# Attention's 32 bodies written as a hardware loop of seven passes and a tail of four

## The reference

```python
x = L0_attn_x                                  # (2, 2048, 256), float32
xn = _layernorm(x, axis=-1)
x = x + mamba(xn) + ffn(xn)
# inside ffn, with 16 heads of width 16:
scores = jnp.einsum('bhqd,bhkd->bhqk', q, k) / jnp.sqrt(jnp.float32(D))
attn = jax.nn.softmax(scores, axis=-1)
o = jnp.einsum('bhqk,bhkd->bhqd', attn, v)
x = x + (o @ wo + bo)
hn2 = _layernorm(x, ln2_g, ln2_b).reshape(-1, h)
idx = jnp.argmax(hn2 @ gate_w + gate_b, axis=-1)
moe = y[idx, jnp.arange(hn2.shape[0])]         # y: relu feed-forward of each of 8 experts
```

## Time and profile before

| | |
|---|---|
| median of 3 executions | 3217.68 us (3217.47 to 3218.07) |
| the profiled execution | 3217.68 us |
| its span, first to last instruction | 3215.9 us |
| instructions in it | 37482 |
| busy in attention, 1433.7 to 2637.7 us (1204.0 us) | PE 1188.9, DVE 1163.0, ACT 881.5, POOL 80.2 us |
| granted TensorE clock, mean | 0.943 |

### The profile page before, as it was taken

The page is one execution under the profiler, slowest core; times in us unless marked ns, Lnnn a source line. Parts: engine busy times, 40 slices in busy tenths (PEclk is TensorE's granted clock), DMA queues, the critical chain, the costliest instruction groups (busy, mean ns, idle before and its releaser), DMA issues. The chain is left out here.

```text
span 3215.9 us, 37482 instructions
## 1 busy us (share of the span) xinstructions
PE 2883.6 (90%) x13148; PEld 1472.8 (46%) x13148; DVE 2647.9 (82%) x4268; ACT 1706.1 (53%) x2088; POOL 981.1 (31%) x554
## 2 busy tenths in 40 slices
PE   5768899898898775899999999999999998859998
PEld 3423344343343332444444444444444442648887
DVE  8819999999999996799999999999999994642222
ACT  3435564565655632067777777777777777101111
POOL 3506565565565565101101101011010000344443
PEclk9889999999999987599999999999999999769999
DMA  7731121221221222835555545555554420655663
GB/s 202 182 104 60 63 83 72 80 84 60 74 89 68 73 72 30 109 46 74 84 71 78 77 62 75 67 82 84 71 77 63 63 31 29 96 137 193 202 210 107
DMA packets 206598, 288.18 MB, mean 90 GB/s; under 512 B 113437, under 2 KB 154038, under 8 KB 191948
## 3 DMA queue, kind: packets, MB, share of 16 engines
q1 hardware_dynamic: 195052, 260.22, 39.1%
q0 software_dynamic: 11360, 25.62, 2.7%
HBM read 237.34 MB, written 53.36 MB: 90 GB/s over the span
## 5 line engine op out<-in xcount | busy, mean ns | idle before, releaser
L782 DVE TENSOR_REDUCE attn_mx<-attn_pX 128x1 f32<-128x512 f32 (+1 forms) x2560 | 1305.0, 576 | 72.5 <-PE attn_pX L687 32.2
L758 ACT ACTIVATE attn_pr<-attn_pS 128x1024 f32<-128x1024 f32 x1024 | 991.6, 1021 | 447.1 <-PE attn_pS L699 447.0
L687 PE MATMUL attn_pX<-attn_ks,attn_qs 48*128 48x512 f32 (+1 forms) x2560 | 899.7, 439 | 46.2 <-DMA attn_vs<-v_d 25.0
L687 PEld LDWEIGHTS attn_pX<-attn_ks,attn_qs 48*128 48x128 f32 x2560 | 446.7, 189 | 667.6 <-DVE attn_mx L782 562.7
L1221 PE MATMUL mamba_pY<-mamba_g,mamba_ident 128*128 128x512 f32 x1024 | 520.1, 655 | 136.7 <-DVE mamba_g L1369 136.5
L699 PE MATMUL attn_pS<-attn_qs,attn_ks 50*128 50x512 f32 x2048 | 626.0, 437 | 3.6 <-ACT attn_pr L758 3.6
L1349 DVE TENSOR_TENSOR_SCAN mamba_h<-mamba_pA,mamba_hs,mamba_db 128x512 f32<-128x512 f32 x512 | 616.9, 1263 | 13.5 <-ACT mamba_pA L1071 13.2
L1007 POOL TENSOR_TENSOR mamba_db<-mamba_bq,mamba_u 128x2048 f32<-128x2048 f32 x128 | 580.2, 4533 | 63.2 <-DVE mamba_u L1310 63.2
L1071 ACT ACTIVATE mamba_pA<-mamba_dt,held_an 128x512 f32<-128x512 f32 x512 | 352.5, 691 | 389.6 <-DVE mamba_h L1349 389.1
L709 PE MATMUL attn_pO<-attn_pr,attn_vs 128*17 128x512 f32 x4096 | 542.4, 601 | 0.8 <-ACT attn_pr L758 0.7
L1221 PEld LDWEIGHTS mamba_pY<-mamba_g,mamba_ident 128*128 128x128 f32 x1024 | 202.9, 207 | 442.6 <-DVE mamba_g L1369 225.0
(11 more groups left out here) (200 smaller groups left out, 2100.1 us busy)
## 6 DMA issues: line engine op xcount, KB each, us to landing
mamba_bq<-bc_d SPq DMA_DIRECT2D x64, 1024.0 KB, 4.7
attn_ks<-parts_d SPq DMA_DIRECT2D x192, 256.0 KB, 9.4
exp_w<-in_w SPq DMA_DIRECT2D x46, 1024.0 KB, 5.7
attn_vs<-v_d SPq DMA_DIRECT2D x32, 544.0 KB, 15.9
parts_d<-proj_qp SPq DMA_DIRECT2D x32, 512.0 KB, 5.8
attn_qs<-parts_d SPq DMA_DIRECT2D x192, 64.0 KB, 8.4
oraw_d<-attn_oe SPq DMA_DIRECT2D x32, 256.0 KB, 2.1
v_d<-proj_vs SPq DMA_DIRECT2D x32, 136.0 KB, 4.9
```

The source lines that it names most:

```text
L687: pe.matmul(pX[bank(s, e)][:, 0:width], QS[slot][rows, pair, qt * P:(qt + 1) * P], KS[slot][rows, pair, keys:keys + width], start=True, st ...
L758: act.activation(PR[2 * (kt % 2) + pair][:, :, :], pS[pair][:, :, :], ACT.Exp, scale=HD ** -0.5).then_inc(p_sb, 1)
L782: dve.tensor_reduce(MX[:, col, a:a + 1], pX[bank(s, e)][:, 0:width], AX.X, ALU.max).then_inc(x_max, 1)
```

## The change

In `phase_attention` the 32 calls of `body` that were written out for each engine become a hardware loop, one for each engine, of NI / RING - 1 = 7 passes with four bodies each, and the last four bodies written out behind it. In the loop i is a register of the engine, so that every threshold with i in it, and every DMA address, is computed from it when the program runs. `left` is 9 there, which stands for "three or more are left and it is not the third last". The loops of the engines are not joined to each other; they are held together by the same semaphores as before.

```diff
         def bodies(eng, body):
 
-            for n in range(NI):
-                body(n // RING, n % RING, NI - 1 - n)
+            if NI > RING:
+                with eng.Fori(0, NI // RING - 1) as i:
+                    for s in range(RING):
+                        body(i, s, 9)
+            for s in range(RING):
+                body(NI // RING - 1, s, RING - 1 - s)
```

## The result

The changed kernel takes 3247.6 us (median of 4, 3243.0 to 3251.3) against 3217.6 before (3214.2 to 3218.1): ratio 1.0101, 95% interval 1.0087 to 1.0115, so 28 to 37 us slower. The forecast was 3245. The time came out as forecast. The account has the place of the cost right, and two of its terms wrong in size, one too low and one too high.

What follows compares the result with a forecast made beforehand. PE and DVE together were taken to pace attention. 3217.7 + 21 (jumps) + 2.8 (`turned`) + 4.5 (thresholds) = 3246, given as 3245 us; own range 3230 to 3261, 8 in 10 range 3227 to 3272.

Steps and rivals of the forecast that it cites:

- What bounds attention: Attention's key tile loop: PE and DVE together set the pace through three pX banks, 2.64 us a period; ACT has slack.
- PE's jump, 3.5 us: PE's jump back at a pass's end: code fetched anew, 3.5 us each, counting nearly whole on the path.
- DVE's, 2.9, with 2.1 left on the path: DVE's jump back: 2.9 us, some 0.8 covered by queued reductions, 2.1 left; it lies beside PE's jump.
- The term of the jumps, 6 x 3.5 = 21 us: Six jumps back in the attention loop, priced at PE's 3.5 us each: 21 us, range 12 to 27.
- if PE's stall were gone, DVE's 2.1 us would be next: At a jump, without PE's stall, the uncovered 2.1 us of DVE's jump would be the next cost.
- The thresholds, 4.5 us: Register step before each wait in the loop: 0.01 us for each of 448 key tiles, 4.5 us.
- `turned`, 2.8: Two waits ahead of the transpose at `turned`: about 0.1 us on DVE's path in 28 bodies, 2.8 us (0 to 6).
- ACT's jump, 2.5 us beside PE's: ACT's jump back at a pass's end: code not kept, 2.5 us as in mamba's loop, beside PE's jump.
- PE's pass of 10.5 blocks is not kept: PE's looped attention pass, about 2700 instructions or 10.5 blocks, is fetched anew at each jump.
- cheap jumps: Rival (same): all six jumps cost the 0.3 us PE showed in mamba, thresholds hidden; 3222 us, chance 0.10.
- Register steps on PE's path: Rival (slower still): steps around the scores delay them and the values start later, 29 us; 3270 us, chance 0.17.
- Scores out of the way: Rival (faster): scores issued later leave PE to the key block, 27 us less; 3215 or 3194 us, chance 0.05.

Runs made afterwards that it cites:

- the hint: Changed kernel with a branch prefetch hint at the head of each pass on each engine; ratio 1.0049 to the kernel before.
- the fill: Changed kernel with four matmuls of zeros queued on PE at the end of each pass, ahead of its jump; ratio 1.0094 to the kernel before.
- the run with passes of 656: Changed kernel with eight bodies in a pass, three passes, eight bodies written out: two jumps in place of six; ratio 1.0039 to the kernel before.
- the run with a pass of some 1930: Changed kernel with values multiplied for one head of four, shortening PE's pass; ratio 1.0124 to the kernel before, the same cut written out 1.0012.
- the first run: Changed kernel with six loops of one pass each, nothing to jump back to, registers for 24 bodies, eight written out; ratio 1.0016 to before.
- the hint on PE and DVE: Changed kernel, loop on all engines, with the branch prefetch hint on PE and DVE only; ratio 1.0018 to the kernel before.
- the last run: Kernel before with 25 matmuls of zeros at attention's start and a small one behind each block ahead of the first body; ratio 1.0271.

## Why the prediction was right

- *What bounds attention, and that a loss at either engine is lost for good*: held. Gaps of 0.6 us under the hint made bodies 0.6 to 0.7 us longer, and 3.7 us of stall under the fill made them 3.7 longer.
- *PE's jump, 3.5 us*: 3.6. *DVE's, 2.9, with 2.1 left on the path*: 2.8 to 2.9, and 2.4. They lie side by side, as forecast: both together cost no more than either alone.
- *The term of the jumps, 6 x 3.5 = 21 us*: mis-sized. Its stall is right at 6 x 3.7 = 22; the half clock that follows is missing. By the times a jump costs about 5.0 us, six 30. For the same reason "if PE's stall were gone, DVE's 2.1 us would be next" had the right engine and the wrong price: DVE's alone makes 31 us.
- *The thresholds, 4.5 us, and `turned`, 2.8*: mis-sized the other way by the profile. Together about 2 us in the bodies, 2.5 by the line through two and six jumps; the choice of 0.01 us a key tile was too high by these. The run without jumps, at 5 us (2 to 9), doesn't exclude 7. The two errors, some 9 us too low and 5 too high, nearly cancel. That the time came within 3 us is in part luck.
- *ACT's jump, 2.5 us beside PE's*: 0.3. The forecast took ACT's pass to be about as long as mamba's or longer, and so not kept; it is shorter, 329 instructions against 372, and the run with passes of 656 had the long jump. It costs nothing either way.
- *PE's pass of 10.5 blocks is not kept*: held. Of the 2048 instructions that the Trainium skill gives as PE's store (Runtime: NRT & Kernel Launch, Instruction fetch mechanics), the run with a pass of some 1930 does not bear out that such a pass is kept.
- The rivals: cheap jumps are what the hint makes, and the loop then costs 6 us. Register steps on PE's path are refuted by the first run. Scores out of the way didn't occur; no body got shorter than 43.0 us.

## What to carry to other kernels

Before a phase is rolled up, look for the engines that pace it and count the instructions of a pass on each. A pass longer than what the engine keeps pays a fetch at each jump, 3.6 us on PE and 2.8 on DVE here, and if PE then stands still, the clock may go with it. Make few jumps, or hint those of the pacing engines alone, and compare the granted clock body by body: in the profile of the changed kernel stalls of 3.4 to 3.8 us made their bodies 5 to 10 us longer.

## What the runs showed of the hardware

- In the 28 bodies of all profiles PE was idle for 1.2 to 3.8 us in 27 places, and each time the clock went to its lower level for 3.4 to 20.5 us, of different length in the same kernel (13.7, 13.7, 17.1, 6.8, 6.8, 6.8 us at the six jumps of the changed kernel). What sets the length is open. Two idle times were shorter than these and longer than 0.5 us: one of 0.7 us was followed by 6.8 us at the lower level (the run without jumps), one of 0.8 us was not (the hint on PE and DVE). The many of 0.5 us or less, 0.3 to 0.4 at most hinted jumps, were not.
- A PE that is busy by its records can stay at the lower level: 153.6 us in the last run.
- PE's wait for code shows as a COMPARE_BRANCH of 3.3 to 3.8 us in the changed kernel, DVE's as a gap of 2.8 to 2.9 us behind one of 63 ns.
- Passes that were kept and not, by records: PE 1132 kept, 1866 and 2634 not; ACT 329 kept, 372 and 656 not; SP 185 kept, 363 not; DVE 391 and 674 not.
